# A graph layer and a feed-forward layer in one kernel: the first product taken in pairs of tiles by seven half-size products, and edge ranks counted from chunk to chunk

## What is computed

```python
x = x + gnn(layernorm(x))           # h = u @ W.T + b; out[i] = sum over edges (i, j) of dis[i]*dis[j]*h[j]
x = x + ffn(layernorm(x))           # base product + shared low rank + routed low rank (top 2 of 6, softmax gate)
deg = 1 + (number of edges with src == i); dis = deg ** -0.5
```

## Time and profile before

| | us |
|---|---|
| median of 3 runs (2184.4 to 2184.64) | 2184.49 |
| the profiled execution | 2184.77 |
| its span, first to last instruction | 2182.9 |
| PE busy | 2129.1 (98%) |
| DVE busy | 1537.7 (70%) |
| ACT busy | 522.6 (24%) |
| POOL busy | 633.3 (29%) |

### The profile page before, as it was taken

One profiled execution on the slowest core, in us unless ns is written; L12 is line 12 of the kernel. 1 busy time (PEld: TensorE's weight loads), 2 busy tenths in 40 slices (PEclk: granted clock), 3 DMA queues, 4 the chain that ended last, 5 costly groups with the idle time before them and its releaser, 6 DMA issues.

```text
span 2182.9 us, 33549 instructions
## 1 busy us (share of the span) xinstructions
PE 2129.1 (98%) x11577; PEld 1966.5 (90%) x11577; DVE 1537.7 (70%) x3709; ACT 522.6 (24%) x888; POOL 633.3 (29%) x773
## 2 busy tenths in 40 slices
PE   7999999999999999949999999999999999999999
...
GB/s 215 193 126 145 135 126 145 129 132 137 128 141 135 126 144 174 158 174 150 163 150 160 157 150 167 158 149 165 152 159 157 146 171 154 148 166 152 159 125 39
DMA packets 107463, 325.23 MB, mean 149 GB/s; under 512 B 28576, under 2 KB 28912, under 8 KB 107206
## 3 DMA queue, kind: packets, MB, share of 16 engines
...
## 4 chain that ended last, share of the span: by engine, by line
PE 92%; DVE 4%; issue 2%; POOL 1%; DMA 1%; ACT 0%; DVEq 0%; POOLq 0%; ACTq 0%
PE bo L664 27%; PE bo L666 27%; PE bo L665 27%; PE bt L672 6%; PE bo L787 2%; PE bo L791 2%; PE bo L789 2%; DVE acc L1036 1%; DVE acc L1044 1%; DVE st L1046 0%; PE bt L781 0%; DVE z_lo L1115 0%; POOL g L556 0%; DMA g<-h_rows,row_now 0%; DVE acc L1071 0%
## 5 line engine op out<-in xcount | busy, mean ns | idle before, releaser
L664 PE MATMUL bo<-base_hi,z_hi 128*128 128x380 f32 (+1 forms) x1896 | 654.7, 345 | 5.1 <-issue 5.1
L665 PE MATMUL bo<-base_lo,z_hi 128*128 128x380 f32 (+1 forms) x1896 | 639.2, 337 | 0.0
L666 PE MATMUL bo<-base_hi,z_lo 128*128 128x380 f32 (+1 forms) x1896 | 639.0, 337 | 0.0
L664 PE MATMUL bo<-w_hi,u_hi 128*128 128x512 f32 x1264 | 500.3, 396 | 3.9 <-issue 3.2
L666 PE MATMUL bo<-w_hi,u_lo 128*128 128x512 f32 x1264 | 493.5, 390 | 0.0
L665 PE MATMUL bo<-w_lo,u_hi 128*128 128x512 f32 x1264 | 492.8, 390 | 0.0
L664 PEld LDWEIGHTS bo<-base_hi,z_hi 128*128 128x128 f32 x1896 | 358.8, 189 | 5.5 <-issue 5.5
L665 PEld LDWEIGHTS bo<-base_lo,z_hi 128*128 128x128 f32 x1896 | 359.0, 189 | 0.0
L666 PEld LDWEIGHTS bo<-base_hi,z_lo 128*128 128x128 f32 x1896 | 357.5, 189 | 0.0
L556 POOL DMA_INDIRECT g<-h_rows,row_now x237 | 307.5, 1297 | 91.2 <-issue 91.2
L664 PEld LDWEIGHTS bo<-w_hi,u_hi 128*128 128x128 f32 x1264 | 238.1, 188 | 51.7 <-issue 4.1
...
## 6 DMA issues: line engine op xcount, KB each, us to landing
...
```

What stands on the lines that cost most here:

```text
L664: nc.tensor.matmul(ps, hi[:, k, :], m_hi[:, k, n], start=(k == 0), stop=False)
L665: nc.tensor.matmul(ps, hi[:, k, :], m_lo[:, k, n], start=False, stop=False)
L666: return nc.tensor.matmul(ps, lo[:, k, :], m_hi[:, k, n], start=False, stop=(ends and k == KB - 1))
```

## The change

The first seven tiles (`HEAD`) stay as they were. The other 72 go in 36 pairs (`PAIRS`). Of a pair, the two tiles are the upper and lower half of a 256x1024 left operand, which is cut into four quarters A11, A12 (first tile, left and right half of its columns) and A21, A22 (second tile); the weight is cut into four quarters too. Winograd's form of Strassen's scheme gives the four quarters of the result (C11, C12 for the first tile, C21, C22 for the second) from seven products of quarters instead of eight. Their left operands are A11, A12, A22 and the sums S1 = A21+A22, S2 = S1-A11, S3 = A11-A21 and S4 = A12-S2; the right operands are B11, B21, B22 and four sums T1 to T4 of weight quarters, made once during the head on POOL (`quarter`) and split on ACT and DVE. Each product is 4 blocks x 3 matmuls of 128x512.

The results need sums as well. ACT copies the product of A11 (`p1`); POOL adds the bias halves to it (`p1_right`, `p1_left`); DVE adds products and these in `partial` and `eviction`; ACT scales each quarter by `dis` in `weigh_part` and the own rows by `sqd` in `own_rows`; POOL adds the two in `rest`. There is one `un` where there were two.

Ranks: in place of comparing each chunk with all the earlier ones, a table `counts` in DRAM holds how often each source was seen. For each chunk POOL gathers the counts of its 128 sources (`counts_of`), adds the ranks within the chunk, and scatters the new counts back (`count_chunk`), two chunks a pair from pair 2. The ranks within a chunk are made on DVE by `ranks(p)`, four chunks in each of the first ten pairs. The base weight is loaded, on ACT's queue, and split only in and after the last pair.

```diff
-COMPARED = 16
-RANK_AT, SCATTER_AT, BASE_AT = 4, 58, 68
+HEAD = 7
+PAIRS = (TILES - HEAD) // 2
+A11, S2, A12, S3, S1, A22, S4 = range(7)
+B11, T2, B21, T3, T1, T4, B22 = range(7)
+LEFT_ORDER = {A11: 1, A12: 2, S2: 3, S3: 4, S1: 5, A22: 6, S4: 7}
+BANK, BEGINS = (0, 1, 0, 1, 2, 1, 2), (True, True, False, False, True, False, False)
+C11, C22, C21, C12 = range(4)
+PARTS = ((0, 0), (1, 1), (1, 0), (0, 1))
+RANKED = 4
+COUNT_AT, SLOT_AT, SCATTER_AT, TABLE_AT = 2, 22, 23, 28
...
+            def quarter(into, a, c, of):
+                for k in range(4):
+                    nc.gpsimd.tensor_tensor(into[:, k, :], a[:, k, :], c[:, k, :], ALU.subtract) \
+                        .then_inc(t_ok, 1)
...
+            def rest(p, t, vs, ok):
+                for v in vs:
+                    pool.wait_ge(weighed, part_at(p, v))
+                pool.wait_ge(xs_ok, 2 * p + t + 1)
+                xt = xn[(first(p) + t) % 6]
+                nc.gpsimd.tensor_tensor(xt[:], xt[:], hrow[t][:], ALU.add).then_inc(ok, 1)
+            def counts_of(c):
+                if c == 0:
+                    pool.wait_ge(zero_stored, 48)
+                else:
+                    pool.wait_ge(count_put, 16 * c)
+                carry_wait(0 + c % 2)
+                nc.gpsimd.indirect_dma_start(
+                    counted[:, c:c + 1], None, count_dram,
+                    bass.IndirectOffsetOnAxis(ap=src_u[:, c:c + 1], axis=0),
+                    bounds_check=NPAD + 2 * P - 1, oob_is_err=True).then_inc(count_in, 16)
+            def count_chunk(c):
+                if c % RANKED == 0:
+                    pool.wait_ge(ranked, c // RANKED + 1)
+                pool.wait_ge(count_in, 16 * (c + 1))
+                nc.gpsimd.tensor_tensor(count[:, c:c + 1], counted[:, c:c + 1], nth[:, c:c + 1],
+                                        ALU.add).then_inc(count_ok, 1)
+                carry_wait(2 + c % 2)
+                nc.gpsimd.indirect_dma_start(
+                    count_dram, bass.IndirectOffsetOnAxis(ap=count_to[:, c:c + 1], axis=0),
+                    count[:, c:c + 1], None, bounds_check=NPAD + 2 * P - 1,
+                    oob_is_err=True).then_inc(count_put, 16)
+            for p in range(PAIRS):
+                if p + 1 < PAIRS:
+                    rstd(first(p + 1))
+                pool.wait_ge(p1_ok, p + 1)
+                if p > 0:
+                    pool.wait_ge(c_ok, part_at(p - 1, C21))
+                nc.gpsimd.tensor_tensor(p1_right[:], p1[:], b_rows[:, half(1)], ALU.add) \
+                    .then_inc(p1_right_ok, 1)
+                if p + 1 < PAIRS:
+                    rstd(first(p + 1) + 1)
+                nc.gpsimd.tensor_tensor(p1_left[:], p1[:], b_rows[:, half(0)], ALU.add) \
+                    .then_inc(p1_left_ok, 1)
+                chunks = [c for c in range(2 * (p - COUNT_AT), 2 * (p - COUNT_AT) + 2)
+                          if 0 <= c < CHUNKS]
+                if chunks:
+                    counts_of(chunks[0])
+                if p > 0:
+                    rest(p - 1, 0, (C11, C12), ra_ok)
+                if chunks:
+                    count_chunk(chunks[0])
+                    counts_of(chunks[1])
+                    count_chunk(chunks[1])
...
+                rest(p, 1, (C22, C21), rb_ok)
+            rest(PAIRS - 1, 0, (C11, C12), ra_ok)
...
+            def first_halves(p):
+                act.wait_ge(ta_done, 2 * p + 1)
+                if p > 0:
+                    act.wait_ge(done, product_at(p - 1, A11))
+                nc.scalar.activation(left_raw[A11][:], bt[0][:], ACT.Copy).then_inc(a11_ok, 1)
+                act.wait_ge(ta_done, 2 * p + 2)
+                if p > 0:
+                    act.wait_ge(done, product_at(p - 1, A12))
+                nc.scalar.activation(left_raw[A12][:], bt[1][:], ACT.Copy).then_inc(a12_ok, 1)
+                act.wait_ge(a11_ok, p + 1)
+                left_high(A11, left_raw[A11][:])
+                act.wait_ge(a12_ok, p + 1)
+                left_high(A12, left_raw[A12][:])
+            def second_half(p):
+                act.wait_ge(tb_done, 2 * p + 1)
+                if p > 0:
+                    act.wait_ge(s3_ok, p)
+                nc.scalar.activation(a21[:], bt[0][:], ACT.Copy).then_inc(a21_ok, 1)
...
+            def weigh_part(p, v):
+                t, h = PARTS[v]
+                act.wait_ge(c_ok, part_at(p, v))
+                nc.scalar.activation(hrow[t][:, half(h)], hrow[t][:, half(h)], ACT.Copy,
+                                     scale=dis[:, first(p) + t:first(p) + t + 1]) \
+                    .then_inc(weighed, 1)
...
+            for p in range(PAIRS):
...
+                last_sum_high(p)
+                if p > 0:
+                    weigh_part(p - 1, C12)
+                act.wait_ge(done, product_at(p, A11))
+                if p > 0:
+                    act.wait_ge(c_ok, part_at(p - 1, C22))
+                else:
+                    act.wait_ge(t_lo_ok, 16)
+                nc.scalar.activation(p1[:], bp[p % 2][BANK[A11]][:], ACT.Copy).then_inc(p1_ok, 1)
+                if p + 1 < PAIRS:
+                    normalise(first(p + 1))
+                weigh_part(p, C11)
+                own_rows(p, 0)
+                if p == PAIRS - 1:
...
+                if p + 1 < PAIRS:
+                    normalise(first(p + 1) + 1)
+                    first_halves(p + 1)
+                    second_half(p + 1)
+                    sums_high(p + 1)
+                weigh_part(p, C22)
+                own_rows(p, 1)
...
+                if p + 1 < PAIRS:
+                    late_high(p + 1)
+                    last_half_high(p + 1)
+                weigh_part(p, C21)
+            weigh_part(PAIRS - 1, C12)
...
+            def product(p, n):
+                ps = bp[p % 2][BANK[n]][:]
+                for k in range(4):
+                    nc.tensor.matmul(ps, left_hi[n][:, k, :], wr_hi[n][:, k, :],
+                                     start=(BEGINS[n] and k == 0), stop=False,
+                                     skip_group_check=True)
+                    nc.tensor.matmul(ps, left_hi[n][:, k, :], wr_lo[n][:, k, :], start=False,
+                                     stop=False, skip_group_check=True)
+                    last = nc.tensor.matmul(ps, left_lo[n][:, k, :], wr_hi[n][:, k, :],
+                                            start=False, stop=(k == 3), skip_group_check=True)
+                return last
...
+            def transpose_second(p):
+                pe.wait_ge(un_ok, first(p) + 2)
+                pe.wait_ge(a12_ok, p + 1)
+                transposes(un, tb_done)
...
+            for p in range(PAIRS):
+                for n in range(7):
+                    pe.wait_ge(left_hi_ok, left_at(p, n))
+                    pe.wait_ge(left_lo_ok, left_at(p, n))
+                    if n == A12:
+                        pe.wait_ge(p1_ok, p + 1)
+                    if n == S3:
+                        pe.wait_ge(u2_ok, p + 1)
+                    if n == A22:
+                        pe.wait_ge(u3_ok, p + 1)
+                    if n == S4:
+                        pe.wait_ge(c_ok, part_at(p, C22))
+                    product(p, n).then_inc(done, 1)
...
+                    if n == A12 and p + 1 < PAIRS:
+                        transpose_first(p + 1)
+                    if n == S3 and p + 1 < PAIRS:
+                        transpose_second(p + 1)
...
+            def ranks(q):
+                dve.wait_ge(row_in, 16 * (q + 1))
+                link(nc.vector.tensor_copy(row[:].rearrange("p c f -> p (c f)"), row_i[:]))
+                for k in range(RANKED):
+                    c = q * RANKED + k
+                    for of, n in ((earlier_of, nth), (later_of, follow)):
+                        link(nc.vector.scalar_tensor_tensor(
+                            same_src[:], row[:, k, :], srcs[:, c:c + 1], of[:],
+                            ALU.is_equal, ALU.mult, accum_out=n[:, c:c + 1]))
+                cs = slice(q * RANKED, (q + 1) * RANKED)
+                link(nc.vector.tensor_scalar(nth[:, cs], nth[:, cs], 1.0, None, ALU.add))
+                link(nc.vector.tensor_scalar(follow[:, cs], follow[:, cs], 0.5, None, ALU.is_lt))
+                link(nc.vector.tensor_scalar(slot[:, cs], srcs[:, cs], spare[:], None,
+                                             ALU.subtract))
+                link(nc.vector.tensor_tensor(slot[:, cs], slot[:, cs], follow[:, cs], ALU.mult))
+                nc.vector.tensor_scalar(count_to[:, cs], slot[:, cs], spare[:], None, ALU.add) \
+                    .then_inc(ranked, 1)
...
+            def eviction(p, v, n, other, ok):
+                t, h = PARTS[v]
+                dve.wait_ge(done, product_at(p, n))
...
+                    dve.wait_ge(part_stored[v], 16 * p)
+                    dve.wait_ge(rb_ok if t else ra_ok, p)
+                if ok is not None:
+                    dve.wait_ge(ok, p + 1)
```

(53 more changed lines are left out.)

651 lines of the change are left out of this document (446 added, 205 removed).

## The result

The changed kernel takes 2383.46 us in the median (2381.7 to 2386.2, 4 runs) against 2184.44 before: a ratio of 1.0913, 95% interval 1.0894 to 1.0932. Forecast were 2282 us and a range of 2205 to 2345. The direction was right, the size was half of what came: +199 instead of +98. The profiled execution spans 2379.9 us, 197 more than before.

The account below looks back on a forecast made before the run. PE bounded the old kernel; in the changed one, waits through DVE, ACT and POOL would bind each pair. Pairs 89.6, head 7 and between the stages 1 added to 2184.8 gave 2282 us, range 2205 to 2345.

Parts of the forecast that it names:

- What PE saves: PE in a pair: 84 matmuls instead of 96, 20.9 us; over 36 pairs 98 us, the most to win.
- Prices: Time per instruction on DVE, ACT and POOL, such as POOL additions at 2.4 us for 1024 and 1.25 for 512.
- power 0.55: POOL's power instruction, counted twice in a pair, ahead of `p1_right` and of `p1_left`: 0.55 us each.
- The ring: Waits tying DVE, ACT and POOL together from C11 of one pair to C11 of the next: 23.8 us.
- POOL ... 8.5, frees `hrow[0]`: Last part of a pair's chain of waits: POOL's additions and powers, 8.5 us, ending in the `rest` C11 waits for.
- The sum: Whole kernel: 89.6 us longer over the pairs, head 7, between the stages 1, giving 2282 us.
- the rival's 2 us a pair: PE's clock falls to 1.2 GHz in waits: 2 us and more in 20 pairs, 2323, up to 2360; chance 0.16, shared with upper-end additions.
- the main case: Pairs bound by the chain of waits through DVE, ACT and POOL with slow POOL additions: 2282 us, chance 0.60 (2255 to 2310).
- 4.7 us, less the 0.2 of slack, 4.5: `ranks(p)` on DVE ahead of C12 and the statistics: 4.5 us added to the chain of waits in pairs 1 to 10.
- Between the stages: DVE's low parts of the base weight mostly hidden by the 28.3 us gather wait; `rest` and one hand-over add 1 us.
- Head: Start up to the first pair: waits for S1 to S4, low parts and `finish_rows` ahead of the first partial sum, +7 us.
- the middle case: Whole kernel: the forecast time of 2282 us, with slow POOL additions and no fall of the clock.

Follow-up runs that it names:

- ACT's order: Changed kernel with `weigh_part(p, C11)` and `own_rows(p, 0)` moved behind `second_half(p + 1)` on ACT: 2245.0 us, 1.0277.
- the fillers' kernel: Changed kernel with 16 extra unused matmuls on PE ahead of the second transposes of pairs 2 to 21: 2362.5 us, 1.0817.
- The experiment on its order: Changed kernel with POOL's T3 quarter behind tile 6's rstd and T1's low parts behind the first pair's sums: 2384.5 us, 1.0926.

## Why the prediction was wrong, point by point

- **What PE saves** (20.9 a pair) was right: pairs take it wherever PE binds.
- **Prices** were right, with one exception: POOL 2.40 and 1.29, four round trips within POOL's pause, but the second "power 0.55" took 0.99, which is the whole of 24.2 against 23.8. The ring was right too. The step "POOL ... 8.5, frees `hrow[0]`" was a link, not the cause: the same ring opens by ACT's order.
- **The sum left the clock out** and gave it to a rival: 1.5 us in pairs with counts, 0.9 with ranks, 21 us in all. That was smaller than the rival's 2 us a pair, and it came on top of the main case. Treating it as an alternative was the error. It rested on a misreading: "No wait between 0.5 and 5 us at full clock is in this trace" is false. In stage 2 of the kernel before, PE works at full clock, waits 1.71 us and drops to half speed within a microsecond of starting again (0.17 us from one matmul of 380 columns to the next at first, then 0.32):

```profile
1004.53 0.36 PE L787 MATMUL bo<-bl_hi,hs_hi 113*128 113x262 f32 x1 [1.71 <-DVE hs_lo L1138]
...
1006.47 0.52 PE L664 MATMUL bo<-base_hi,z_hi 128*128 128x380 f32 x1
```

```profile
1004.50:1010.00 5.50, 5.47 (x24) 5.50 (x25) 4.20 (x5) 0.00 (x0) 3.78 (x6) 0.69 0.99 215
```

- **Ranks** were mis-sized: for "4.7 us, less the 0.2 of slack, 4.5" the fillers' kernel has 6.5, since the first comparison stands 2.1 us beside POOL's addition. With the 0.9 of the clock, pairs with ranks and counts took 33.2 instead of 30.1, some 25 us in all.
- **`slot_table`** was put at nothing, without a reason. It takes DVE 5.5 us (2.40 of them for one small operation beside POOL's addition), and its pair took 30.1 instead of 23.8.
- **Between the stages** "+1" was wrong by 26: I costed DVE's low parts and took the load of b_low, which before lies at the start of the kernel, for one like the others. Cut in two it gives 25 of them back in PE's wait, 20 in the kernel's time.
- **Head** "+7" was 19. The prediction had no row of PE, ACT and POOL there side by side, and priced DVE's low parts as if POOL's quarters did not run beside them (some 3 us). The experiment on its order found no gain, so the rest stays open.
- **The range** ended at 2345, since only one of these could be added to the middle case. That the direction came out right was no luck: the ring that gives PE's saving back is the one in the trace.
